# A routed expert layer: the first matrix of each tile's expert as the stationary operand, fetched per tile

## What is computed

```
x0   = du_dt(x)                          # stencil with zX, zY, zR
x1   = x0 + attention(layernorm(x0))     # 16 heads of 16, causal over the 16 sequences
hn2  = layernorm(x1)
rp   = softmax(hn2 @ router_w.T)         # 8 experts
topw, topi = top_k(rp, 2)
hmid = gelu(einsum('th,ehf->tef', hn2, w1), approximate=False)     # w1: 8 x 256 x 512
y    = einsum('tef,efh->th', hmid * gates[:, :, None], w2)         # w2: 8 x 512 x 256
out  = x + x1 + y                        # 4096 tokens of 256
```

## Time and profile before

| | us |
|---|---|
| median of 3 runs (range) | 738.69 (736.26 to 738.71) |
| profiled execution | 738.08 |
| its span, first to last instruction | 736.3 |
| PE busy | 610.8 (83%) |
| POOL busy | 465.0 (63%) |
| DVE busy | 429.7 (58%) |
| ACT busy | 348.7 (47%) |

### The profile page before, as it was taken

One profiled execution on the slowest core, in us unless ns is written; L12 is line 12 of the kernel. 1 busy time (PEld: TensorE's weight loads), 2 busy tenths in 40 slices (PEclk: granted clock), 3 DMA queues, 4 the chain that ended last, 5 costly groups with the idle time before them and its releaser, 6 DMA issues. The chain is left out here.

```text
span 736.3 us, 10160 instructions
## 1 busy us (share of the span) xinstructions
PE 610.8 (83%) x2640; PEld 401.8 (55%) x2640; DVE 429.7 (58%) x1028; ACT 348.7 (47%) x814; POOL 465.0 (63%) x562
## 2 busy tenths in 40 slices
PE   2677889683776978869989799999699999999992
PEld 1233444443444655646656557667476767666661
DVE  1256568883999988863895697989943100111110
ACT  4334442421433645436776355666356555444440
POOL 5776567788678762775678885584365853443442
PEclk9688887966788997989999789999989999999998
DMA  4366654123212320342323422243234644444332
GB/s 124 122 212 196 208 170 114 44 82 97 48 44 59 74 60 13 81 95 42 65 40 83 106 30 31 45 88 66 43 76 69 127 85 66 66 66 73 61 56 25
DMA packets 51547, 59.83 MB, mean 81 GB/s; under 512 B 7386, under 2 KB 47075, under 8 KB 51428
## 3 DMA queue, kind: packets, MB, share of 16 engines
q0 software_dynamic: 18288, 23.28, 19.8%
q1 hardware_dynamic: 33204, 35.91, 17.2%
HBM read 35.89 MB, written 27.46 MB: 86 GB/s over the span
## 5 line engine op out<-in xcount | busy, mean ns | idle before, releaser
L979 PE MATMUL b_y<-w_s,hm_hmT 128*128 x568 | 135.6, 382 | 11.1 <-ACT y L548 10.3
L446 POOL DMA_INDIRECT out_dram<-y,xin x71 | 117.1, 1650 | 34.2 <-issue 29.7
L964 PE MATMUL b_h<-w_s,xT 128*128 x284 | 135.0, 598 | 1.6 <-ACT xT L509 1.6
L979 PEld LDWEIGHTS b_y<-w_s,hm_hmT 128*128 128x128 f32 x568 | 102.8, 191 | 25.0 <-issue 13.9
L1056 PE MATMUL b_qk<-wqkv,hT 128*128 128x512 f32 x128 | 94.1, 876 | 0.0
L910 DVE TENSOR_TENSOR pv_prod<-kv,pr 128x1024 f32<-128x1024 f32 (+2 forms) x80 | 82.4, 1072 | 20.0 <-PE b_at L1100 19.9
L681 DVE TENSOR_SCALAR y<-b_y,xin,live 128x256 f32<-128x256 f32 x24 | 13.1, 544 | 137.2 <-PE b_y L979 137.2
L844 DVE TENSOR_TENSOR qk_prod<-q,kv 128x1024 f32<-128x1024 f32 (+2 forms) x80 | 88.2, 1126 | 7.8 <-ACT kv L578 6.9
L1100 PE MATMUL b_at<-ident,pv_prod 128*128 128x128 f32 x544 | 74.5, 287 | 18.4 <-DVE pv_prod L910 17.4
L414 POOL DMA_INDIRECT xs_d<-ring,slot_row x64 | 72.7, 1136 | 19.1 <-issue 18.2
L852 DVE TENSOR_REDUCE sc<-qk_prod 128x64 f32<-128x1024 f32 (+2 forms) x80 | 82.1, 1051 | 0.3
(11 more groups left out here) (166 smaller groups left out, 1019.8 us busy)
## 6 DMA issues: line engine op xcount, KB each, us to landing
xin<-xs_d SPq DMA_DIRECT2D x71, 132.5 KB
w_s<-in_L_ffn_w_dram SPq DMA_DIRECT2D x16, 512.0 KB, 4.4
xp<-in_x_dram SPq DMA_DIRECT2D x32, 128.0 KB
xud<-in_x_dram SPq DMA_DIRECT2D x32, 128.0 KB
out_dram<-x POOLq DMA_DIRECT2D x32, 128.0 KB, 3.3
xud<-in_x_dram SPq DMA_DIRECT2D x32, 126.0 KB
out_dram<-y,xin POOLq DMA_INDIRECT x71
xud<-in_x_dram SPq DMA_DIRECT2D x64, 1.0 KB
```

Of the source, the lines that this page charges most:

```text
L446: pool.indirect_dma_start(out_rows, bass.IndirectOffsetOnAxis(ap=xin[:, j % NX, H:H + 1].bitcast(U32), axis=0), y[:, j % NY, :], None, com ...
L964: mm = pe.matmul(b_h[:, :], xT[:, k * P:(k + 1) * P], w1_s[:, bass.ds(e * (HC * F) + k * F, F)], start=(k == 0), stop=(k == HC - 1))
L979: mm = pe.matmul(b_y[:, 0:H], hmT[:, k * P:(k + 1) * P], w2_s[:, bass.ds(e * (FC * H) + k * H, H)], start=(k == 0), stop=(k == FC - 1))
```

## The change

The first matrix of a tile's expert becomes the stationary operand and `xT` the moving one. For each of four blocks of 128 hidden units two products of 128 columns add up to a 128x128 piece that has the hidden units on the partitions: the transposed hidden layer. Gelu writes it straight to `hmT`. `turn_h` on PE, its copy on ACT, and `hm` are gone. The banks `b_h` and `b_t` now both take hidden layers, tile by tile in turn, and `xT` and `hmT` have two buffers each.

The first matrices are no longer held. SP fetches that of tile j's expert, 512 KB, with `weights_in(j)` right after `tile_in(j)`, into one of four buffers `w1_t`; the buffer is free when the up product of tile j-4 is done, which it waits for by `h_ready`. The preload in steps 1 to 8 is gone, and that of `w2_s` starts in step 1. PE waits per tile for its matrix, and for the gelu of tile j-2 before it writes the bank again.

The order in a slot changes too: on PE `turn_in(j+2)` comes first, then the reading of tile j's expert number, `up(j+1)` and `down(j)`; on ACT `xT` of j+2 comes first, then the result of j-1 and gelu of j+1.

```diff
-        w1_s = sb("w1_s", [P, E * HC * F])
+        w1_t = sb("w1_t", [P, NW, HC * F])
...
-        xT = sb("xT", [P, HC * P])
-        hm_hmT = sb("hm_hmT", [P, 2 * F])
-        hm, hmT = hm_hmT[:, 0:F], hm_hmT[:, F:2 * F]
+        xT = sb("xT", [P, 2, HC * P])
+        hmT = sb("hmT", [P, 2, F])
...
+        h_banks = (b_h, b_t)
...
-        W1_FROM = 1
-        W2_FROM = 3
+        W2_FROM = 1
...
+            def weights_in(j):
+
+                if j >= NW:
+                    sp.wait_ge(s["h_ready"], j - NW + 1)
+                e = sp.value_load(tab[0:1, j:j + 1], min_val=0, max_val=E - 1)
+                sp.dma_start(w1_t[:, j % NW, :].rearrange("p (k f) -> p k f", k=HC),
+                             w1[bass.ds(e, 1), :, :].rearrange("o (k p) f -> p (o k) f", p=P)).then_inc(w1_in[j % NW], 16)
...
                 if j + 3 < ALL:
                     tile_in(j + 3)
+                    weights_in(j + 3)
...
             def gelu(j):
                 act.wait_ge(s["h_ready"], j + 1)
-                act.activation(hm[:, :], b_h[:, :], ACT.Gelu).then_inc(s["gelu_done"], 1)
-
-            def turned_h(j):
-                act.wait_ge(s["hT2_ready"], j + 1)
-                act.activation(hmT[:, :], b_t[:, :], ACT.Copy).then_inc(s["hmT_sb"], 1)
+                if j >= 2:
+                    act.wait_ge(s["y_ready"], j - 1)
+                act.activation(hmT[:, j % 2, :], h_banks[j % 2][:, :], ACT.Gelu).then_inc(s["gelu_done"], 1)
...
-            def up(j, e):
+            def up(j):
+                pe.wait_ge(w1_in[j % NW], 16 * (j // NW + 1))
                 pe.wait_ge(s["xT_sb"], j + 1)
-                for k in range(HC):
-                    mm = pe.matmul(b_h[:, :], xT[:, k * P:(k + 1) * P], w1_s[:, bass.ds(e * (HC * F) + k * F, F)],
-                                   start=(k == 0), stop=(k == HC - 1))
+                if j >= 2:
+                    pe.wait_ge(s["gelu_done"], j - 1)
+                for f in range(FC):
+                    for k in range(HC):
+                        mm = pe.matmul(h_banks[j % 2][:, f * P:(f + 1) * P], w1_t[:, j % NW, k * F + f * P:k * F + (f + 1) * P],
+                                       xT[:, j % 2, k * P:(k + 1) * P], start=(k == 0), stop=(k == HC - 1))
                 mm.then_inc(s["h_ready"], 1)
...
             def slot(j):
                 if j == -1:
-                    pe.wait_ge(s["w1_in"], 16 * E)
                     pe.wait_ge(s["w2_in"], 16 * E)
                     turn_in(0, 0, 1)
...
                 if j + 2 < ALL:
                     turn_in(j + 2, (j + 2) % NX, (j + 2) // NX + 1)
                 if j >= 0:
-                    down(j, loaded.pop(j))
+                    if j in FIRST:
+                        pe.wait_ge(s["tab_ready"], group_of(j) + 1)
+                    e = expert(j)
+                if j + 1 < ALL:
+                    up(j + 1)
+                if j >= 0:
+                    down(j, e)
```

More of the change, by code:

```diff
@@ L53, in adaln_moe_block @@
     NPV = 3
+    NW = 4
     ctx = ExitStack()
@@ L152, in adaln_moe_block @@
             rt_sub rt_exp rt_m rt_cum rt_cum_sb slots_ready tab_ready pre_ready
-            x_tr xT_sb h_ready gelu_done hT2_ready hmT_sb y_ready y_sb pre_done
+            x_tr xT_sb h_ready gelu_done y_ready y_sb pre_done
             dve_chain pool_chain""".split()
@@ L157, in adaln_moe_block @@
         x1_added = [sem(f"x1_added{i}") for i in range(4)]
+        w1_in = [sem(f"w1_in{i}") for i in range(NW)]
         xin_in = [sem(f"xin_in{i}") for i in range(NX)]
@@ L308, in tile_in @@
                 sp.dma_start(xin[:, j % NX, :], xs_d[bass.ds(row, P), :]).then_inc(xin_in[j % NX], 16)
+            def weights_in(j):
[4 more added lines that the diff above has]
+                             w1[bass.ds(e, 1), :, :].rearrange("o (k p) f -> p (o k) f", p=P)).then_inc(w1_in[j % NW], 16)
             def slot(j):
                 if j == -1:
-                    tile_in(0)
-                    tile_in(1)
+                    for i in range(2):
+                        tile_in(i)
+                        weights_in(i)
                 if j + 3 < ALL:
                     tile_in(j + 3)
+                    weights_in(j + 3)
             def place(g, n):
@@ L529, in turned_in @@
                 act.wait_ge(s["x_tr"], j + 1)
-                affine(xT, b_x, 1).then_inc(s["xT_sb"], 1)
+                affine(xT[:, j % 2, :], b_x, 1).then_inc(s["xT_sb"], 1)
             def gelu(j):
                 act.wait_ge(s["h_ready"], j + 1)
-                act.activation(hm[:, :], b_h[:, :], ACT.Gelu).then_inc(s["gelu_done"], 1)
-            def turned_h(j):
-                act.wait_ge(s["hT2_ready"], j + 1)
-                act.activation(hmT[:, :], b_t[:, :], ACT.Copy).then_inc(s["hmT_sb"], 1)
+                if j >= 2:
+                    act.wait_ge(s["y_ready"], j - 1)
+                act.activation(hmT[:, j % 2, :], h_banks[j % 2][:, :], ACT.Gelu).then_inc(s["gelu_done"], 1)
             def result(j):
@@ L553, in slot @@
                     turned_in(0)
-                else:
-                    turned_h(j)
+                if j + 2 < ALL:
+                    if j >= 0:
+                        act.wait_ge(s["h_ready"], j + 1)
+                    turned_in(j + 2)
                 if 0 <= j - 1 < TAIL:
@@ L959, in expert, with down @@
                 return pe.value_load(tab[0:1, j:j + 1], min_val=0, max_val=E - 1)
-            def up(j, e):
+            def up(j):
+                pe.wait_ge(w1_in[j % NW], 16 * (j // NW + 1))
                 pe.wait_ge(s["xT_sb"], j + 1)
-                for k in range(HC):
-                    mm = pe.matmul(b_h[:, :], xT[:, k * P:(k + 1) * P], w1_s[:, bass.ds(e * (HC * F) + k * F, F)],
-                                   start=(k == 0), stop=(k == HC - 1))
+                if j >= 2:
[4 more added lines that the diff above has]
+                                       xT[:, j % 2, k * P:(k + 1) * P], start=(k == 0), stop=(k == HC - 1))
                 mm.then_inc(s["h_ready"], 1)
-            def turn_h(j):
+            def down(j, e):
                 pe.wait_ge(s["gelu_done"], j + 1)
-                for k in range(FC):
-                    mm = pe.transpose(b_t[:, k * P:(k + 1) * P], hm[:, k * P:(k + 1) * P], ident[:, :])
-                mm.then_inc(s["hT2_ready"], 1)
-            def down(j, e):
-                pe.wait_ge(s["hmT_sb"], j + 1)
                 if j >= 1:
@@ L978, in down @@
                 for k in range(FC):
-                    mm = pe.matmul(b_y[:, 0:H], hmT[:, k * P:(k + 1) * P], w2_s[:, bass.ds(e * (FC * H) + k * H, H)],
+                    mm = pe.matmul(b_y[:, 0:H], hmT[:, j % 2, k * P:(k + 1) * P], w2_s[:, bass.ds(e * (FC * H) + k * H, H)],
                                    start=(k == 0), stop=(k == FC - 1))
                 mm.then_inc(s["y_ready"], 1)
-            def next_expert(j):
-                if j in FIRST:
-                    pe.wait_ge(s["tab_ready"], group_of(j) + 1)
-                return expert(j)
-            loaded = {}
             def slot(j):
                 if j == -1:
-                    pe.wait_ge(s["w1_in"], 16 * E)
                     pe.wait_ge(s["w2_in"], 16 * E)
                     turn_in(0, 0, 1)
-                if j >= 0 and j not in loaded:
-                    loaded[j] = expert(j)
-                if j + 1 < ALL:
-                    e_next = loaded[j + 1] = next_expert(j + 1)
-                if j >= 0:
-                    turn_h(j)
-                if j + 1 < ALL:
-                    up(j + 1, e_next)
                 if j + 2 < ALL:
```

8 lines of the change are left out of this document (1 added, 7 removed).

## The result

The changed kernel takes **761.76 us** (median of 4 runs, 757.39 to 767.37) against 737.86 for the kernel before on the same chip (736.26 to 738.71): a ratio of 1.033, 95% interval 1.026 to 1.039. It is slower by 24 us, where 732.0 was forecast with a range of 722 to 747. The profiled execution took 761.88, its span is 760.1.

A forecast was written before the change was run, and what follows sets the result against it. In the last stage PE, 4.10 us a tile, was taken to lead the add loop by 0.36 us. Mixed stage -2.5, 554 to 592.7 us nothing, tail -3.5: together -6, 732 us, range 722 to 747.

The forecast's parts named there:

- The up product: PE's tile slot: sixteen records of 128 columns take 1.76 us, so the slot lasts 3.71 us, 0.39 less.
- Rival D: PE's up product: weight loads aren't hidden, slot 4.45 to 5.0 us, total 752 to 774; chance 0.05.
- the adds take over as the bound: Last stage: POOL's adds into `out`, 3.93 us a tile, set the pace above PE's 3.71.
- rival A: Last stage: adds aren't lengthened by weight loads, tail 121.6 us, total 726; chance 0.20.
- the add lengthened by 0.3 us: Last stage: each waiting add with a weight load beside it lands 0.3 us later, 4.55 us apart instead of 4.25.
- The rule of the Trainium skill: DMA engines drain one queue's whole packet before another's; by it an add loses 0 or 1.7 us, not 0.3.
- rival B: Last stage: adds lengthened by 0.8 us or more, both transfers triggered by the same landing; total 745; chance 0.20.
- The mixed stage: -2.5 forecast: 180 to 554 us: 7.5 of 12 us saved PE work counts, less 5 for late `xin`, giving -2.5.
- I put nothing: Mixed stage: loads of `x` stand 1.1 us longer behind the fetch in SP's queue, priced at no cost.
- The transposes at the slot's head: PE's order: `xin`'s transposes come 2.16 us earlier, so late `xin` costs 5.6 to 7.2 us; 5 counted.
- 554 to 593 us: nothing forecast: From 554 to 592.7 us POOL's adds interleaved with scatters, at 4.56 us, are the bound; nothing gained.
- Rival E: Last stage: PE waits in every slot and its clock falls; counted in (B)'s chance.

The follow-up runs named there:

- e6: Changed kernel with matrices fetched only for tiles 0 to 3 and `xin`'s transposes back behind the up product: 724.5 us, 0.980 of the kernel before.
- e4: Changed kernel with the old slot order, `xin`'s transposes behind the up product and `xT` behind gelu: 755.7 us, 1.020 of the kernel before.
- e2: Kernel before, old product and order, but each tile's first matrix fetched and used as moving operand: 754.6 us, ratio 1.019.
- e7: Changed kernel with each tile's matrix fetch issued ahead of its `xin` load instead of behind it: 788.6 us, 1.066 of the kernel before.
- e8: e4 with each tile's matrix fetch issued ahead of its `xin` load: 763.2 us, 1.034 of the kernel before.
- e10: e4 with the matrix fetches issued by ACT at the head of its slot instead of SP: 761.1 us, 1.029 of the kernel before.
- e5: Changed kernel fetching only half of each matrix, 256 KB, used for both halves of the product: 747.0 us, 1.011 of the kernel before.
- e11: Changed kernel with matrices fetched only for tiles 0 to 30, later ones using what the buffers hold: 743.6 us, 1.006 of the kernel before.
- e1: Changed kernel with matrices fetched only for tiles 0 to 3, new slot order kept: 735.8 us, 0.996 of the kernel before.
- e12: Changed kernel with the attention steps' loads of `x` issued by ACT one step ahead instead of SP: 778.4 us, 1.053 of the kernel before.
- e13: Kernel before with the attention steps' loads of `x` issued by ACT one step ahead instead of SP: 763.9 us, ratio 1.033.
- e9: Kernel before, but for tiles 36 to 70 DVE copies the resident first matrix into buffers as stationary operand, without fetches: 732.0 us, ratio 0.990.

## Why the prediction was wrong

**Right: the product and what bounds the tail.** The up product was priced at 1.76 us and the slot at 3.71; where PE does not stand (e6) they take 1.78 and 3.73. Rival D (weight loads not hidden) is out. That the adds take over as the bound is what the kernel after shows. Where nothing is fetched, the tail is 121.2 us (e6), and rival A's working said 121.6.

**The step that failed: the add lengthened by 0.3 us.** The mechanism was named and its price taken from the nearest row, adds of `x1` beside two loads ahead of each. It measured 0.84 us on the mean (5.19 less 4.35), inside the two bounds of 0 and 1.67. Put into the sum, 20 x 0.54 more makes the tail 138.7 instead of 127.9; it was 140.4. The 0.3 took every add to have one matrix beside it. For fourteen of the twenty that was nearly the size, 0.43 (4.83 less 4.40). The other six, second behind a free add, meet two matrices and took 1.80 more (6.04 less 4.24). e4 and e2 show the same two groups, 4.76 and 6.18, 4.67 and 6.39. The sum counted the free adds as a gain and not that two landings in a row start two matrices.

The rule of the Trainium skill that the prediction weighed ("DMA: Bandwidth & Descriptors", Queues, rings and completion order) was read as 0 or 1.7 us for an add. The trace neither bears this out nor refutes it: the fourteen lie between 4.22 and 6.12 us, eleven of them below 5. Moving the matrix forward (e7, e8) or to another queue (e10) did not bring 4.35 back. Nor is a common start of add and load the reason, though the prediction gave it as rival B's ground: in e10 the fetches follow no landing, and the mean is 5.17.

The mean of 0.84 is rival B's price of 0.8, and B had a chance of 0.20. That is in part luck, since B too has every add alike. Its total of 745 is 17 short, since other terms failed as well.

**The mixed stage: -2.5 forecast, +9.0 measured.** Of 12 us of PE work saved, 7.5 were counted on the path. e6, which has the saving and none of the costs, reaches add 28 at 556.1 against 555.6 before, and needs 2.8 us less for the steps 20 to 31 (187.4; it lost some 4 us in the first ten steps, where no tile runs). So 3 to 4 us were on the path, not 7.5; that DVE and POOL set the pace there for most of the time is my reading of the earlier trace rows, not shown by a run. The first ten steps are a matter of the execution: kernels that are alike up to there took 109.1 (e5) to 113.1 us (e11) for them.

The 8.0 us lost from step 20 to 31 can be taken apart by the same copies of `aT`: -2.8 for the product (e6, 187.4, less before, 190.2), +5.6 for the order (e1, 193.0, less e6) and +5.2 for the transfers (after, 198.2, less e1). Each is one execution; two of the same program in these steps, after and e11, took 198.2 and 197.4. The step that failed besides the 7.5 is the last term, put at nothing. The loads of `x` behind the fetch, for which "I put nothing", may be most of it (e12), but e10 does not agree, so this stays open. POOL's wait for them grew from 4.8 to 14.2 us. The groups by line of the kernel after:

```profile
L395 POOL COPY xp<-xp 128x2 f32<-128x2 f32 x32 | 10.8, 336 | 14.2 <-DMA xud<-in_x_dram 14.2
...
L960 PE MATMUL b_x<-ident,xin 128*128 128x128 f32 x142 | 29.1, 287 | 21.0 <-DMA xin<-xs_d 19.2 <-ACT xT L516 1.6
```

Waits of 4.8 and 5.4 us now were no ground for nothing: the slack of SP's queue was not looked at, only its waits.

**The transposes at the slot's head: about the right size.** 5 us were put into the sum, of 5.6 to 7.2 priced, all in the mixed stage. The order costs 6.1 us in the kernel after (less e4), 3.8 of them before add 28 and 0.9 in the tail. Without fetches it is 11.3 (e1 less e6), of which the tail has 5.2, where nothing was put. PE's 12.8 us for `xin` in the last stage are no cost of the order: in e4 PE waits as long, for the matrix.

**554 to 593 us: nothing forecast, +5.7 measured.** Adds interleaved with scatters were taken as a fixed 4.56 us. They are adds that wait like the others and lengthen with traffic: 41.0 us from add 28 to 38 before, 38.0 in e6, 46.6 after. I should have carried the lengthening over to this stretch.

**Rival E, hardly seen.** The granted clock stayed at 0.97 to 1.00 in the last stage, as expected. In 450 to 500 us it fell from 1.00 to 0.93 while PE's busy time went from 49.21 to 45.63; no run isolates what that cost.

Together, as book-keeping by stage: the lengthening 10.8 in the tail and 1.7 that it leaves over there, 5.7 in the adds between scatters, 11.5 in the mixed stage. On top of the forecast's -6 that is the 24 us. What stays open is how the DMA engines divide their time between an add and a load, and so why one matrix costs 0.43 us and two cost 1.80.

## What to carry to other kernels

Before streaming something that was resident, find the loop that consists of small dependent transfers, and go through its links in order of time: how many of the new loads fall beside each? Here one load cost a link 0.43 us and two cost it 1.80, and two came wherever the loop had made a quick step. An average share of DMA time shows none of this. Halving the bytes helped (e5); issuing the load earlier or from another engine did not (e7, e8, e10). A saving on the busiest engine is worth what the second loop leaves, here 10.2 us over the 32 tiles of the tail (131.4 less 121.2), 0.32 of 0.39 a tile, and it turns negative if the change feeds the second loop. A queue's wait can also be what paces it: taking it out let sixteen preloads go at once (e13). When only the operand's form is wanted, a copy by an idle engine from the resident data can give it without any transfer (e9).

## What the runs showed of the hardware

- An accumulating indirect DMA of 128 rows, 4.35 us from one to the next when each waits for the landing before, takes 4.66 with 256 KB and 5.19 with 512 KB loaded beside it, whether SP (5.19) or ACT (5.17) issues the load. With SP issuing 512 KB, adds with one such load beside them take 4.83, the second add behind a free one, with two beside it, 6.04.
- f32 products of 128 columns with new weights for each record run at 0.111 us a record (sixteen in 1.78), the pace of the columns.
- Sixteen loads of 512 KB issued in a row, from 13.0 to 43.9 us (e13), landed 12.1 us after their issue at the median instead of 4.4 (before), and ACT waited up to 8.2 us for the small loads of `x` issued meanwhile. From 30 to 50 us the core's DMA engines moved 356 to 375 GB/s. The page of e13:

```profile
w_s<-in_L_ffn_w_dram SPq DMA_DIRECT2D x16, 512.0 KB, 12.1
```

The first attention step came 15 us later than before. The other 9 us of e13's 24 are not explained by a run; some of them may be ACT's issuing.
